# Zero rows under the matmuls of a two-head attention, and two copies written as sums

## The reference, cut to what matters

```python
scores = jnp.einsum('bhqd,bhkd->bhqk', Q, K) / scale
mask = _tpms_mask(L, phase, threshold, temperature)
scores = scores + TPMS_WEIGHT * jnp.log(mask + 1e-06)[None]
attn = jax.nn.softmax(scores, axis=-1)
out = jnp.einsum('bhqk,bhkd->bhqd', attn, V)
```

## Time and profile before

| | us |
|---|---|
| median of three runs | 2300.82 (2299.14 to 2301.23) |
| the profiled execution's own time | 2312.02 |
| its span, first to last instruction | 2310.2 |
| busy in it: PE, DVE, ACT, POOL | 1905.7, 1503.5, 1163.1, 1083.9 |
| mean granted TensorE clock | 0.848 |

### The profile page before, as it was taken

How to read it: one execution, slowest core, us unless ns; L and a number is a source line. 1 busy time by engine, 2 the same in 40 slices (tenths; PEclk the granted TensorE clock), 3 DMA queues, 4 the chain that set the end, 5 groups by cost and what they waited for, 6 DMA issues and landing times.

```text
span 2310.2 us, 40993 instructions
## 1 busy us (share of the span) xinstructions
PE 1905.7 (82%) x14045; PEld 1105.1 (48%) x14108; DVE 1503.5 (65%) x2433; ACT 1163.1 (50%) x2538; POOL 1083.9 (47%) x871
## 2 busy tenths in 40 slices
PE   4899999769999988569999986399569999884696
PEld 2555565323333333246555553288234554533585
DVE  6788877367777777368887864588445455427486
ACT  3676667346666656346667664244332332334242
POOL 3656665546666657346666550523223133005223
PEclk8999999956666666579999997599779999996798
DMA  6000000120000002000000003200400000000202
GB/s 226 2 2 2 2 2 2 36 69 20 19 19 19 20 18 50 10 1 2 2 2 2 2 2 109 82 19 22 151 0 0 1 0 0 1 0 24 66 23 70
DMA packets 46013, 63.38 MB, mean 27 GB/s; under 512 B 9185, under 2 KB 35553, under 8 KB 45121
## 3 DMA queue, kind: packets, MB, share of 16 engines
q1 hardware_dynamic: 41312, 51.96, 7.3%
q0 software_dynamic: 4544, 9.35, 1.3%
HBM read 45.26 MB, written 21.18 MB: 29 GB/s over the span
## 4 chain that ended last, share of the span: by engine, by line
PE 34%; DVE 8%; ACT 7%; issue 6%; POOL 1%; DMA 1%; DVEq 0%; SPq 0%; ACTq 0%; POOLq 0%
PE PS L1881 3%; PE PS L1863 2%; ACT arena L664 2%; PE PS L1865 2%; PE PS L1864 2%; PE PS L470 1%; PE PS L2506 1%; PE PS L1871 1%; PE PS L2477 1%; PE PS L2523 1%; PE PS L2519 1%; DVE arena L801 1%; PE PS L2453 1%; PE PS L504 1%; PE PS L2527 1%
## 5 line engine op out<-in xcount | busy, mean ns | idle before, releaser
L1655 POOL TENSOR_TENSOR arena<-arena 128x1024 f32<-128x1024 f32 x128 | 300.0, 2353 | 170.1 <-ACT arena L1533 170.0
L664 ACT ACTIVATE arena<-PS,arena 128x128 f32<-128x128 f32 x512 | 180.6, 370 | 117.8 <-DVE arena L828 117.4
L1004 POOL TENSOR_TENSOR arena<-arena 128x512 f32<-128x512 f32 x128 | 132.7, 1041 | 225.1 <-DVE arena L835 223.3
L1585 DVE TENSOR_REDUCE arena<-PS 128x2 f32<-128x1024 f32 x128 | 156.4, 1222 | 76.9 <-PE PS L1463 74.8
L340 PE MATMUL PS<-arena_r 128*128 128x512 f32 x216 | 119.1, 551 | 93.2 <-DVE arena_r L2076 43.2
L1533 ACT ACTIVATE arena<-PS 128x1024 f32<-128x1024 f32 x128 | 130.8, 1023 | 126.7 <-PE PS L1487 126.6
L801 DVE SCALAR_TENSOR_TENSOR arena<-PS,fcol,big 128x512 f32<-128x512 f32 x256 | 177.3, 741 | 14.4 <-PE PS L342 7.8
L2187 POOL DMA_INDIRECT expert_y<-arena x78 | 74.7, 958 | 200.4 <-DVE arena L2146 151.1
L1550 ACT ACTIVATE arena<-arena 128x1024 f32<-128x1024 f32 x128 | 134.4, 1051 | 19.7 <-DVE arena L1607 18.6
L987 POOL TENSOR_TENSOR arena<-arena 128x512 f32<-128x512 f32 x64 | 109.3, 1708 | 64.8 <-ACT arena L640 29.4
L640 ACT ACTIVATE arena<-PS 128x512 f32<-128x512 f32 x128 | 74.3, 594 | 111.1 <-PE PS L342 76.6
(11 more groups left out here) (379 smaller groups left out, 4791.5 us busy)
## 6 DMA issues: line engine op xcount, KB each, us to landing
big<-in_gu SPq DMA_DIRECT2D x16, 512.0 KB, 7.5
sorted_x<-in_slots SPq DMA_DIRECT2D x2, 2515.5 KB, 15.9
arena<-sorted_x SPq DMA_DIRECT2D x6, 774.0 KB, 7.3
big<-in_dn SPq DMA_DIRECT2D x16, 256.0 KB, 8.2
arena<-expert_y SPq DMA_DIRECT2D x16, 256.0 KB, 3.3
arena<-q_split SPq DMA_DIRECT2D x96, 32.0 KB
arena<-k_split SPq DMA_DIRECT2D x96, 32.0 KB
heads_out<-arena SPq DMA_DIRECT2D x128, 16.0 KB
```

What stands on the lines that cost most here:

```text
L664: act.activation(pr[:, u % 2, t, :], PS[:, u % 2, t * P:(t + 1) * P], ACT.Exp, bias=nmax[:, u % 2, t:t + 1], accum_out=psum_[:, u % 2, t:t ...
L1004: g.tensor_tensor(pn[:, u % 2, :, :], pr[:, u % 2, :, :], pinv[:, u % 2, :].unsqueeze(2).broadcast_to([P, TPB, P]), ALU.mult).then_inc(s(" ...
L1585: v.tensor_reduce(a_nmax[:, st % 2, PAIR * half:PAIR * half + PAIR], PS[:, 0:PAIR, :], AX.X, ALU.max, negate=True).then_inc(s("a_nmax"), 1)
L1655: g.tensor_tensor(a, a, mk[:, hp, PAIR * half:PAIR * half + PAIR, :], ALU.mult).then_inc(s("a_masked"), 1)
```

## The change

Three matmuls contract over more rows: `score` over 64, `shifted` over all 128, `argument` over all 128. For that the POOL program fills all of `mq_st`, `mk_st`, `q_st` and `k_st` with zeros first, and then k's rows 64 and 65 with ones: five memsets for each head, ten in all, in place of six. SP's wait for these memsets moves ahead of the first loads of mask factors. On DVE, the cast into `hi` and the copy of v into `v_head` become sums with a column of zeros that is broadcast along the free dimension.

```diff
--- before.py
+++ after.py
@@ -1409,11 +1409,11 @@
                         r = OUT_ROWS * t + w * HD
                         sp.dma_start(o_dram[w, bass.ds(h * HD, HD), :, t * P:(t + 1) * P], o_sb[r:r + HD, hp, :, :]).then_inc(s("o_stored%d" % hp), 16)
 
+            sp.wait_ge(s("head_pads"), START + 5 * HEADS_PER_PASS)
             for hp in range(HEADS_PER_PASS):
                 load_mask_factors(0, hp)
             sp.wait_ge(s("parts0_stored"), START + 192)
             sp.wait_ge(s("parts1_stored"), START + 192)
-            sp.wait_ge(s("head_pads"), START + 6)
             for hp in range(HEADS_PER_PASS):
                 load_head(0, hp)
             sp.wait_ge(s("mask_clamped"), START + TPB)
@@ -1460,14 +1460,14 @@
                     pe.wait_ge(s("a_nmax"), START + at(i, MAX_OPS * STEPS, MAX_OPS * st + (1 if half else 2 - MAX_OPS)))
                 for k in range(PAIR):
                     t = PAIR * half + k
-                    mm = pe.matmul(PS[:, k, :], q_st[hp][0:KS, b, t * P:(t + 1) * P], k_st[hp][0:KS, b, :], start=True, stop=True)
+                    mm = pe.matmul(PS[:, k, :], q_st[hp][0:ROW_MAX, b, t * P:(t + 1) * P], k_st[hp][0:ROW_MAX, b, :], start=True, stop=True)
                 mm.then_inc(s("a_scores"), 1)
 
             def argument(i, q, bank):
                 hp, tile = q // TPB, q % TPB
                 if tile == 0:
                     pe.wait_ge(s(f"factors{hp}_loaded"), START + at(i, 32, 32))
-                pe.matmul(PS[:, bank, :], mk_st[hp][0:MF, tile * P:(tile + 1) * P], mq_st[hp][0:MF, :], start=True,
+                pe.matmul(PS[:, bank, :], mk_st[hp][:, tile * P:(tile + 1) * P], mq_st[hp][:, :], start=True,
                           stop=True).then_inc(s("mask_arg"), 1)
 
             def turn_max(i, st, clamped):
@@ -1484,7 +1484,7 @@
                 pe.wait_ge(s("a_exp"), START + at(i, 2 * STEPS, max(2 * (st - 1) + half + 1, 0) if type(i) is int and i == 0 else 2 * (st - 1) + half + 1))
                 for k in range(PAIR):
                     kt = PAIR * half + k
-                    mm = pe.matmul(PS[:, 2 + kt, :], k_st[hp][0:KX, b, kt * P:(kt + 1) * P], q_st[hp][0:KX, b, :], start=True, stop=True)
+                    mm = pe.matmul(PS[:, 2 + kt, :], k_st[hp][:, b, kt * P:(kt + 1) * P], q_st[hp][:, b, :], start=True, stop=True)
                 mm.then_inc(s("a_shifted"), 1)
 
             def values(i, st):
@@ -1590,7 +1590,7 @@
                 if not (type(i) is int and i == 0 and st < 2):
                     v.wait_ge(s("max_turned"), START + at(i, STEPS, st - 1))
                 v.wait_ge(s("a_nmax"), START + at(i, MAX_OPS * STEPS, MAX_OPS * st + 2))
-                v.tensor_copy(hi, m).then_inc(s("a_nmax"), 1)
+                v.tensor_tensor(hi, m, c_zero.broadcast_to([P, TPB]), ALU.add).then_inc(s("a_nmax"), 1)
                 v.wait_ge(s("a_nmax"), START + at(i, MAX_OPS * STEPS, MAX_OPS * st + 3))
                 v.tensor_tensor(lo, m, hi, ALU.subtract).then_inc(s("a_nmax"), 1)
 
@@ -1611,7 +1611,8 @@
                 h = i * HEADS_PER_PASS + hp
                 v.wait_ge(s("a_pv"), START + used)
                 plain_wait(v)
-                v.tensor_copy(v_head[:, hp, :, 0:HD], v_all[:, :, bass.ds(h * HD, HD)]).then_inc(s("v_head_ready"), 1)
+                v.tensor_tensor(v_head[:, hp, :, 0:HD], v_all[:, :, bass.ds(h * HD, HD)],
+                                c_zero.unsqueeze(2).broadcast_to([P, B * TPB, HD]), ALU.add).then_inc(s("v_head_ready"), 1)
 
             def body(i, st):
                 if exists(i, st + 2):
@@ -1637,7 +1638,7 @@
         def attn_pool(g):
             pads = 0
             for hp in range(HEADS_PER_PASS):
-                for rows, val in ((q_st[hp][DH // 2:ROW_MAX], 0.0), (k_st[hp][DH // 2:ROW_MAX], 0.0), (k_st[hp][ROW_MAX:KX], 1.0)):
+                for rows, val in ((mq_st[hp], 0.0), (mk_st[hp], 0.0), (q_st[hp], 0.0), (k_st[hp], 0.0), (k_st[hp][ROW_MAX:KX], 1.0)):
                     g.memset(rows, val).then_inc(s("head_pads"), 1)
                     pads += 1
                     g.wait_ge(s("head_pads"), START + pads)
```

## The result

The changed kernel takes 2279.86 us (median of 4 runs, 2249.71 to 2296.64) against 2300.82 before (median of 4): ratio 0.9855, interval 0.9809 to 0.9902. The ratio is of the fast runs alone, without the one of 2296.64; that of the two medians is 0.9909. It is faster, by 21.0 us where 83.8 were forecast.

What follows compares the result with a forecast made beforehand. Mask steps were taken as bound by PE's half clock and VectorE held by GpSimd. Savings 79.0 + 4.1 + 1 - 0.1 = 84 us off 2312.02, less 11.2 to the median, gave 2217 us; range 2168 to 2282.

Steps and rivals of the forecast that it cites:

- the part on rows: Attention's 58 mask steps: wider matmuls lift the clock to 2.4 GHz, 5.64 us a step, saving 79.0 us.
- the price of a held step: Mask steps where GpSimd holds VectorE: 7.1 us, from a 5.25 step plus one copy's lengthening; 8.43 at most.
- the third rival: Mask steps: the clock rises but falls again in held steps where PE idles, half of 79.0 lost; 2261 us, 13%.
- Zero rows count for the clock: Score and mask-argument matmuls: zero rows assumed to count as rows for PE's clock; named the main risk.
- The rival that they count for nothing: Attention matmuls: zero rows, or rows at all, do not count, clock stays at 0.64; 2301 us, 12%.
- How many steps are held: Mask steps: one in four held gives 5.51 us, one behind every short step 5.77; mean taken, 5.64.
- Sums cost and save nothing: VectorE's cast (64 times) and copy of v (16 times) as two-input sums: held just as copies are, 0 us.
- Sums not held: VectorE's two sums: only copies wait for GpSimd, steps reach ACT's 4.84 us; 2171 us, 13%.
- both sums held: Both max_parts operations wait for GpSimd multiplies after each v copy, clock unlifted, 38 us more; 2338 us, 6%.
- The last steps: Steps behind the mask's end: three at half clock drop to 5.14 us each, saving 4.1; bounds 0 and 4.1.
- Before step 1: Six opening mask arguments: the clock may rise within them, saving 1 us; between 0 and 2.
- Memsets: Ten GpSimd memsets for six: 13.3 us with gaps, hidden by idle before k's split, costing 0.1 at most.

Runs made afterwards that it cites:

- e12: Changed kernel with five unread filler matmuls in the odd-numbered (short) steps only; 2226.03 us, ratio 0.9686.
- e11: Changed kernel with five unread filler matmuls in the even-numbered (held) steps only; 2251.09 us, ratio 0.9786.
- e6: e3 with the v operation as a copy again instead of a sum; 2204.45 us, ratio 0.9546.
- e4: Kernel before with maxima reduced straight into one bf16 part, cast and subtraction gone, no other edit; 2270.47 us, ratio 0.988.
- e9: Changed kernel with five unread filler matmuls of 128 rows in each step ahead of turn_max; 2222.22 us, ratio 0.9609.
- e2: Kernel before with the two copies as sums alone, rows as before; 2298.68 us, ratio 1.0004.
- e1: Changed kernel with both sums back as copies, keeping wider rows and ten memsets; 2288.97 us, ratio 0.995.
- e5: e3 with the v operation as a reduce over an axis of one; 2168.01 us, ratio 0.9401.
- e3: Changed kernel with maxima reduced straight into one bf16 part, hi sum and subtraction gone; 2184.18 us, ratio 0.9499.
- e8: e3 with the mask argument back at 6 rows, scores left wide; 2212.2 us, ratio 0.9587.

## Why the prediction was wrong

*The step that failed* is in the part on rows: "I take it that the clock is then 2.4 GHz almost throughout", and with it the price of a held step, 7.1 and not 8.43, "since the rest of the 8.43 was run at 0.60". The 58 steps were to take 327.1 us and took 373.66, at 0.82: 46.6 too many. That zero rows raise the clock and that the holds stay was right; that the raised clock outlives the holds was not, and so a held step was priced too low. At full clock a held step costs 6.88 in the changed kernel, 6.96 in e12 and 7.13 in e11, as forecast; with the clock lost it costs 8.23, or 8.50 with the next step stretched to 5.18. The twelve steps of e11 that keep the clock give 68.44 / 12 = 5.70 us, against the 5.64 that the sum used. The changed kernel's own steps at 1.00 say the same: (4.27 + 6.88) / 2 = 5.58, or 323 for 58. By these two estimates (331 and 323 for the 58 steps) 43 of the missing 46.6 us or all of them were lost to the clock. I had the mechanism in hand, as the third rival (PE idle in held steps), and gave it 13%; the sign that I had written down for it, a clock near 0.8 that falls in held steps, is what came. Its 2261 was the nearest of the rivals by little (2301 lay 21 off), and still 19 short of the time, since it let half of the gain stand, and in the slow pairs nearly all of it goes (6.84 a step against the 7.00 of before). The measured 2279.86 lies inside the range of 2168 to 2282 only because the rivals had widened it; the forecast's own range ended at 2255.

*Zero rows count for the clock*: right, shown by e6 against e4. The rival that they count for nothing is out.

*How many steps are held*: I took the mean of one in four and one behind every short step. The second is what the changed kernel does; the first is what e9 does, once its short steps outlast 4.70. Both cases were rightly reasoned; the mean of them had no ground, and was worth 7.5 us against either.

*Sums cost and save nothing*: right with the rows of before (e2: 1.0004), and not shown with the new ones. But the v operation is held no longer in the changed kernel, 0.29 in the median, nor is it as a copy in e1 (0.23): with the new rows it is the subtraction that waits, for it comes first. "Sums not held" (2171) is out by e2, and "both sums held" happened in a mild form: sum and subtraction wait one behind the other in every second step, at 0.5 to 0.9 and 2.27, but with the clock up it left a gain, as that rival said.

*The last steps*: 4.1 forecast for three of them. They alternate as well and took 6.89, 6.35 and 4.18 for 6.50, 6.87 and 6.50, so 2.4; the one ahead gave 1.0 (4.19 for 5.14), and the one behind took 2.3 back (6.21 for 3.94).

*Before step 1*: 1 forecast, 0.2 measured; the opening arguments did get faster (7.93 for 10.57), and the chain behind them took it back.

*Memsets*: 13.45 for the 13.3 worked out. The split of k began 13.52 behind their start, against 13.30 before, so the idle covered them but for 0.2; 0.1 was the forecast.

*Two readings.* The low stretch in the earlier trace rows is nine slices long, to 982 us, and not eight; nothing was worked out from it. And ACT's 4.84 was taken for a floor, though at 860.81 ACT is busy 4.20 of 4.43 us and PE all of it: in e5 a step takes 4.67 with ACT busy 4.54 of it, so GpSimd's two multiplies were the limit behind the holds. It bears on the rival that gave 2171, not on the forecast.

## What to carry to other kernels

Before a gain from a faster engine is priced by steps at full speed, look at the steps in which that engine waits: here the engine that got its clock back lost it again in many of its waits. Two edits that each give about one per cent gave five together, because one raised the clock and the other took away the idle stretches that dropped it; so try them together before either is thrown out. Where a tiny VectorE operation stands beside long GpSimd work, choose its form by whether it is held (here a reduce was not), and compare the length of the step with GpSimd's work in it.

## What the runs showed of the hardware that was not expected

More matmuls made the kernel faster: five that nobody reads, in each step, took the stage from 373.66 us (394.26 in the run beside it) to 322.03. A held VectorE operation can let GpSimd's gaps pass: the 0.22 us copy at 548.13 spans the end of two multiplies and goes only when the block of five ends, 6.27 us later; six more of e6's copies did so, and the v sum once in e3 (6.37) and four times in e8 (5.79 to 6.53). The Trainium skill ("SBUF — State Buffer", SBUF: two separate sides) says that a GpSimd operation and a VectorE operation that needs the shared pair of ports exclude each other, and that whichever starts first has the pair for its whole instruction. By that the copy would have had 2.35 us to wait at most, an estimate from one multiply; the trace disagrees for these copies and sums, and no run here shows why other holds do end with the next multiply. And the same hold of the subtraction, with PE idle 2.40 us in one step and 2.70 in the other, left the clock at 1.00 in the first and at 0.59 behind the second; from 664 us on every such hold in the 58 steps cost the clock. The length of the idle stretch alone does not decide it: in e12 PE idled 2.46 us ahead of 614.79, in a step at 0.84, and 2.50 ahead of 637.63, in a step at 1.00; in e11 it idled 1.85 in both of the held steps shown, at 0.90 and at 1.00. What does decide was not tried.
